# A graph-attention kernel: the attention transposed by VectorE and DMA instead of TensorE, with the maximum and the exponentials moved to the end of the turn

## What is computed

```python
# layer 0: attention, 8 heads of 64 units, per graph
h = max(layernorm(x), 0)
feats = einsum('bnf,hfu->bhnu', h, W)
dense = e_self[..., :, None] + e_neigh[..., None, :]
dense = leaky_relu(dense, 0.2) + NEG_BIG * (1.0 - A[:, None])
att = softmax(dense, axis=-1)
x = x + relu(einsum('bhij,bhju->bhiu', att, feats) + b)
# layer 1: two hypergraph convolutions
h = max(layernorm(x), 0)
r = relu(hypergraph_conv(h, adj, W1, b1)); r = layer_norm(r, gamma, beta)
x = x + (hypergraph_conv(r, adj, W2, b2) + h)
# hypergraph_conv: Dn * H (Be * H^T (x W^T)) + b, H = (adj != 0)
```

## Time and profile before

| | us |
|---|---|
| median of 3 runs (lowest, highest) | 2488.3 (2486.27, 2489.66) |
| profiled execution: time | 2479.36 |
| profiled execution: span, first to last instruction | 2477.6 |
| PE busy | 2419.2 (98%) |
| DVE busy | 1976.4 (80%) |
| ACT busy | 1763.3 (71%) |
| POOL busy | 1368.0 (55%) |

### The profile page before, as it was taken

How to read it: one execution, slowest core, us unless ns; L and a number is a source line. 1 busy time by engine, 2 the same in 40 slices (tenths; PEclk the granted TensorE clock), 3 DMA queues, 4 the chain that set the end, 5 groups by cost and what they waited for, 6 DMA issues and landing times.

```text
span 2477.6 us, 50428 instructions
## 1 busy us (share of the span) xinstructions
PE 2419.2 (98%) x14004; PEld 2101.6 (85%) x14004; DVE 1976.4 (80%) x4373; ACT 1763.3 (71%) x4489; POOL 1368.0 (55%) x1549
## 2 busy tenths in 40 slices
PE   5799999999999999999999999999999999999997
PEld 3688888888888888888888888888888888888886
DVE  3888888888888888888888888888888888888884
ACT  2677777777777777777777777777777777777774
POOL 2465555565565565565555555555555556556543
PEclk8899999999999999999999999999999999999999
DMA  5344454455445445445445445445454444445442
GB/s 206 95 139 138 136 140 137 134 140 140 134 139 141 134 139 141 134 138 142 132 138 143 131 139 143 125 145 139 128 142 137 134 138 138 137 137 138 138 113 72
DMA packets 656793, 336.69 MB, mean 136 GB/s; under 512 B 554752, under 2 KB 571136, under 8 KB 656768
## 3 DMA queue, kind: packets, MB, share of 16 engines
q1 hardware_dynamic: 636256, 298.64, 43.5%
q10 hardware_dynamic: 20512, 37.76, 4.3%
HBM read 235.03 MB, written 101.26 MB: 136 GB/s over the span
## 4 chain that ended last, share of the span: by engine, by line
PE 95%; DMA 2%; DVE 1%; issue 1%; ACT 1%; POOL 0%; SPq 0%; POOLq 0%; DVEq 0%; ACTq 0%
PE p_w1a L853 15%; PE p_w1a L858 14%; PE p_w1a L854 14%; PE p_att L927 9%; PE p_w1b L854 5%; PE p_w1b L858 5%; PE p_w1b L853 5%; PE p_w1b L957 5%; PE p_att L907 4%; PE p_fa L849 3%; PE p_fa L847 3%; PE p_fa L848 3%; PE p_fb L847 2%; PE p_fb L848 2%; PE p_fb L849 2%; PE p_tb L847 1%
## 5 line engine op out<-in xcount | busy, mean ns | idle before, releaser
L338 POOL TENSOR_TENSOR u<-u,mask 128x1024 f32<-128x1024 f32 x128 | 306.6, 2395 | 761.4 <-DMA u<-en_rows 761.4
L438 ACT ACTIVATE att<-u,shifts 128x128 f32<-128x128 f32 x1024 | 402.3, 393 | 133.0 <-DVE shifts L740 131.6
L853 PE MATMUL p_w1a<-W_hi,rT_hi 128*128 128x512 f32 x1024 | 416.8, 407 | 1.5 <-ACT rT_hi L561 1.5
L854 PE MATMUL p_w1a<-W_lo,rT_hi 128*128 128x512 f32 x1024 | 405.9, 396 | 0.0
L439 ACT ACTIVATE att_low<-u,shifts 128x128 f32<-128x128 f32 x1024 | 399.6, 390 | 0.0
L731 DVE TENSOR_REDUCE neg_max<-u 128x8 f32<-128x1024 f32 x128 | 156.1, 1220 | 149.9 <-POOL u L338 149.9
L858 PE MATMUL p_w1a<-W_hi,rT_lo 128*128 128x512 f32 x1024 | 259.5, 395 | 0.0
L392 POOL TENSOR_TENSOR z_lo<-raw,z_hi 128x512 fp32r<-128x512 f32 x128 | 165.7, 1294 | 154.9 <-ACT z_hi L547 154.9
L927 PE MATMUL p_att<-feats,attT 128*128 128x65 f32 x2048 | 243.1, 272 | 3.1 <-ACT attT L483 3.1
L927 PEld LDWEIGHTS p_att<-feats,attT 128*128 128x128 f32 x2048 | 239.5, 192 | 3.9 <-ACT attT L483 3.9
L547 ACT ACTIVATE z_hi<-raw 128x512 fp32r<-128x512 f32 x128 | 81.1, 634 | 221.6 <-DVE raw L797 221.6
(11 more groups left out here) (121 smaller groups left out, 6759.7 us busy)
## 6 DMA issues: line engine op xcount, KB each, us to landing
u<-en_rows SPq DMA_DIRECT2D x130, 576.0 KB, 3.6
r_blocks<-raw SPq DMA_DIRECT2D x128, 512.0 KB, 2.6
raw<-r_blocks SPq DMA_DIRECT2D x512, 128.0 KB, 3.2
xT_in<-in_xT SPq DMA_DIRECT2D x128, 256.0 KB, 3.9
out<-raw SPq DMA_DIRECT2D x128, 256.0 KB, 2.0
x_in<-in_x ACTq DMA_DIRECT2D x124, 256.0 KB, 3.6
adj_in<-in_adj SPq DMA_DIRECT2D x128, 128.0 KB, 2.5
en_rows<-eT SPq DMA_DIRECT2D x520, 1.1 KB
```

Source lines behind the costliest of these rows:

```text
L338: nc.gpsimd.tensor_tensor(u[:, g.slot(2), 0:HEADS, :], u[:, g.slot(2), 0:HEADS, :], mask[:, :].unsqueeze(1).broadcast_to([P, HEADS, N]), A ...
L438: nc.scalar.activation(att[:, i, :], u[:, g.slot(2), i, :], ACT.Exp, bias=shifts[:, 0, i:i + 1])
L853: mm(dst, hi, w_hi, start=first, stop=False)
L854: mm(dst, hi, w_lo, start=False, stop=False)
```

## The change

The attention of a graph is no longer transposed by PE. DVE transposes all of `att` in 32 x 32 blocks into `attB` (a region of `raw` that otherwise takes the unread result of ACT's square), SP writes that to the DRAM scratch `att_blocks` and loads it back by four DMAs into `attT`, in the shape of the round trip that r already makes. The eight PE transposes and ACT's copy out of PSUM are gone. On SP the write stands at the end of a turn, behind the loads of `rT`, and the four loads stand in the next turn behind `adj_in` and in front of `en_rows`.

On DVE the output and norm of t+1 stand directly behind `rB`; behind them come the new transpose and only then the maximum. `larger` is one instruction for all heads, in front of `rB`. `G_rs` moves from DVE to ACT, behind h. On ACT all sixteen exponentials of t+3 stand at the end of the turn, behind `h0`, which moves there too; `hg_hi` goes in front of `z_hi`. On POOL `rs1`, `beT` and `G_lo` go in front of `rest`. The scores, the mask, the maximum and the features run one turn earlier (t+3 and t+5 in place of t+2 and t+4; features t+4), so AHEAD is 6 and `feats` has four slots. The row of `x` is loaded twice, once for the statistics (`x_in`) and once for the residual (`x_res`).

```diff
-AHEAD = 5
+AHEAD = 6
...
-        x_in = sb("x_in", [P, 4, D])
+        x_in = sb("x_in", [P, 2, D])
+        x_res = sb("x_res", [P, 2, D])
...
+        att_blocks = nc.dram_tensor("att_blocks", [P, HEADS * N], F32, kind="Internal").ap()
+
+        def attB(g):
+
+            return raw[:, 1, 0:DH] if g.loop is None and g.base < 2 else dev
...
-                g = t.plus(4)
+                g = t.plus(5)
                 if g.within(NG) and (g.loop is not None or g.base >= 2):
                     load_xT(g)
                 if t.plus(5).within(NG) and (t.loop is not None or t.base >= -1):
                     load_adj(t.plus(5))
+                g = t.plus(1)
+                if g.within(NG):
+
+                    sp.wait_ge(s_attB_out, g.count(per=16))
+                    for c in range(4):
+                        sp.dma_start(attT[32 * c:32 * (c + 1), :, :].rearrange("a k (q b) -> a k q b", b=32),
+                                     att_blocks.rearrange("(q a) (k c b) -> c a k q b", q=4, c=4, b=32)[c]).then_inc(s_attT, 16)
+                g = t.plus(5)
...
+                g = t.plus(2)
+                if g.within(NG):
+
+                    sp.wait_ge(s_attB, g.count())
+                    sp.dma_start(att_blocks[:, :], attB(g)).then_inc(s_attB_out, 16)
...
-                    if g.plus(2).within(NG):
-                        pool.wait_ge(s_shifts, g.plus(2).count())
+                    if g.plus(3).within(NG):
+                        pool.wait_ge(s_shifts, g.plus(3).count())
...
-            def exps(g, half):
+            def exps(g):
 
                 act.wait_ge(s_shifts, g.count())
                 if g.has(1):
-                    act.wait_ge(s_attT, g.count(1))
-                    act.wait_ge(s_att, g.count(1, per=2))
-                for i in range(half * HH, (half + 1) * HH):
+                    act.wait_ge(s_attB, g.count(1))
+                    act.wait_ge(s_att, g.count(1))
...
             def turn(t):
-                if t.plus(1).within(NG):
-
-                    exps(t.plus(1), 1)
...
-                g = t.plus(1)
-                if g.within(NG):
-
-                    act.wait_ge(s_attT, g.count())
-                    if g.has(1):
-                        act.wait_ge(s_o, g.count(1))
-                    nc.scalar.activation(attT[:, :, :].rearrange("p h n -> p (h n)"), p_att[:, :],
...
+                        act.wait_ge(s_attB_out, g.plus(1).count(per=16) if g.plus(1).within(NG) else g.count(per=16))
                     nc.scalar.activation(dev, r, ACT.Square, bias=nm2[:, :], accum_out=sq2[:, :]).then_inc(s_sq2, 1)
...
-                if t.plus(2).within(NG):
-
-                    exps(t.plus(2), 0)
-                g = t.plus(5)
-                if g.within(NG) and (g.loop is not None or g.base >= 4):
-
-                    act.wait_ge(s_x1, g.count(4))
+
+                def row(g):
                     n = g.base if g.loop is None else g.loop * UNROLL + g.base
-                    act.dma_start(x_in[:, g.slot(4), :], x[bass.ds(n, 1), :, :].rearrange("a p d -> p (a d)")).then_inc(s_in[g.slot(4)], 16)
+                    return x[bass.ds(n, 1), :, :].rearrange("a p d -> p (a d)")
+
+                g = t.plus(7)
+                if g.within(NG) and (g.loop is not None or g.base >= 2):
+
+                    act.wait_ge(s_stats0, g.count(2))
+                    act.dma_start(x_in[:, g.slot(2), :], row(g)).then_inc(s_xin[g.slot(2)], 16)
+                g = t.plus(3)
+                if g.within(NG):
+
+                    if g.has(2):
+                        act.wait_ge(s_x1, g.count(2))
+                    act.dma_start(x_res[:, g.slot(2), :], row(g)).then_inc(s_res[g.slot(2)], 16)
...
+                    act.wait_ge(s_G_sb, g.count())
+                    act.wait_ge(s_rs1, g.count())
+                    if g.has(1):
+                        act.wait_ge(s_hg, g.count(1))
+                    nc.scalar.activation(G_rs[:, :], G[:, g.slot(4), 0:N], ACT.Copy, scale=rs1[:, :]).then_inc(s_G_rs, 1)
...
+                g = t.plus(5)
+                if g.within(NG):
+
+                    act.wait_ge(s_xc, g.count())
+                    if g.has(1):
+                        act.wait_ge(s_feats, g.count(1))
+                    nc.scalar.activation(h0[:, :, 0, :], xc[:, :, :], ACT.Relu).then_inc(s_h0_hi, 1)
+                if t.plus(3).within(NG):
+
+                    exps(t.plus(3))
...
-            def larger(g, half):
-
-                dve.wait_ge(s_exp, g.count(per=2) - 1 + half)
-                heads = slice(half * HH, (half + 1) * HH)
-                nc.vector.tensor_tensor(att[:, heads, :], att[:, heads, :], att_low[:, heads, :], ALU.max).then_inc(s_att, 1)
+            def larger(g):
+
+                dve.wait_ge(s_exp, g.count())
+                nc.vector.tensor_tensor(att[:, :, :], att[:, :, :], att_low[:, :, :], ALU.max).then_inc(s_att, 1)
...
-                if t.plus(1).within(NG):
-                    larger(t.plus(1), 1)
-                g = t.plus(3)
+                g = t.plus(4)
...
+                if t.plus(2).within(NG):
+                    larger(t.plus(2))
...
-                g = t.plus(2)
-                if g.within(NG):
-
-                    dve.wait_ge(s_u, g.count())
-                    nc.vector.reduce_max(neg_max[:, :], u[:, g.slot(2), 0:HEADS, :], X, negate=True).then_inc(s_max, 1)
...
-                    nc.vector.scalar_tensor_tensor(x1[:, s, :], o_sc, 0.0, x_in[:, g.slot(4), :],
+                    dve.wait_ge(s_res[s], g.uses(2, 16))
+                    nc.vector.scalar_tensor_tensor(x1[:, s, :], o_sc, 0.0, x_res[:, s, :],
...
-                    dve.wait_ge(s_G_sb, g.count())
-                    if g.has(1):
-                        dve.wait_ge(s_hg, g.count(1))
-                    dve.wait_ge(s_rs1, g.count())
-                    nc.vector.tensor_scalar(G_rs[:, :], G[:, g.slot(4), 0:N], rs1[:, :], None, ALU.mult).then_inc(s_G_rs, 1)
...
-                if t.plus(2).within(NG):
-                    larger(t.plus(2), 0)
+                g = t.plus(2)
+                if g.within(NG):
+
+                    dve.wait_ge(s_att, g.count())
+                    if g.base == 0:
+                        dve.wait_ge(k_lo1, 1)
+                    if g.has(1):
+                        dve.wait_ge(s_attT, g.count(1, per=64))
+                    if t.within(NG):
+                        dve.wait_ge(s_sq2, t.count())
+                    nc.vector.transpose(attB(g), att[:, :, :].rearrange("p h n -> p (h n)")).then_inc(s_attB, 1)
+                g = t.plus(3)
+                if g.within(NG):
+
+                    dve.wait_ge(s_u, g.count())
+                    nc.vector.reduce_max(neg_max[:, :], u[:, g.slot(2), 0:HEADS, :], X, negate=True).then_inc(s_max, 1)
...
-                g = t.plus(1)
-                if g.within(NG):
-
-                    pe.wait_ge(s_att, g.count(per=2))
-                    if g.has(1):
-                        pe.wait_ge(s_osc, g.count(1))
-                    for i in range(HEADS):
-                        last = nc.tensor.transpose(p_att[:, i * N:(i + 1) * N], att[:, i, :], ident[:, :])
-                    last.then_inc(s_attT, 1)
...
-                    pe.wait_ge(s_attT_sb, g.count())
+                    pe.wait_ge(s_attT, g.count(per=64))
+                    if g.has(1):
+                        pe.wait_ge(s_osc, g.count(1))
                     pe.wait_ge(s_feats_sb, g.count(per=2))
                     for i in range(HEADS):
-                        last = mm(p_o[:, i // HH, i % HH, :], attT[:, i, :], feats[:, g.slot(2), i, :], start=True, stop=True)
+                        last = mm(p_o[:, i // HH, i % HH, :], attT[:, i, :], feats[:, g.slot(4), i, :], start=True, stop=True)
```

More of the change, by code:

```diff
@@ L167, in gnn_two_layers @@
         s_in = [sem(f"s_in{i}") for i in range(4)]
+        s_xin = [sem(f"s_xin{i}") for i in range(2)]
+        s_res = [sem(f"s_res{i}") for i in range(2)]
         s_xT = [sem(f"s_xT{i}") for i in range(2)]
@@ L182, in gnn_two_layers @@
         s_mask, s_max, s_neg_s, s_neg_m, s_shifts, s_att = (sem("s_" + n) for n in ("mask", "max", "neg_s", "neg_m", "shifts", "att"))
-        s_exp, s_attT, s_attT_sb, s_o, s_rden, s_osc, s_x1 = (sem("s_" + n) for n in ("exp", "attT", "attT_sb", "o", "rden", "osc", "x1"))
+        s_exp, s_attB, s_attB_out, s_attT, s_o, s_rden, s_osc, s_x1 = (sem("s_" + n) for n in ("exp", "attB", "attB_out", "attT", "o", "rden", "osc", "x1"))
         s_inc, s_sizes, s_row, s_cnt1, s_inv0, s_inv, s_beT, s_G, s_G_sb = (sem("s_" + n) for n in ("inc", "sizes", "row", "cnt1", "inv0", "inv", "beT", "G", "G_sb"))
@@ L304, in setup_rest @@
                 load_last_piece()
-            turns(sp, turn, NG, {-3: setup_rest})
+            turns(sp, turn, NG, {-4: setup_rest})
             for i in range(2):
@@ L538, in turn @@
                     nc.scalar.activation(h[:, g.slot(2), :], x1[:, g.slot(2), :], ACT.Relu, bias=nm1[:, :]).then_inc(s_h, 1)
```

(13 more changed lines are left out.)

90 lines of the change are left out of this document (40 added, 50 removed).

## The result

The changed kernel takes **2648.4 us** (median of 4 runs, 2642.7 to 2658.9), the kernel before 2487.3 us beside it (2485.0 to 2489.7): a ratio of 1.0653, with an interval of 1.0618 to 1.0688. The forecast was 2413, and 2520 the upper end of its range; the time is that of rival (4), 2648.

A forecast was written before the change was run, and what follows sets the result against it. PE was taken as the bound, 18.59 us a turn; without transposes, and with SP's loop, 17.9. 2479.4 - 127 x 0.69 + 13 = 2405, plus 8.9 for the median: 2413 us; own range 2378 to 2451, eight in ten 2378 to 2520.

The forecast's parts named there:

- rival (4): SP's chain: `attB` and `attT` each pay 1.9 us more, a turn is 19.75 us, 2648 us in all; slower, chance 0.20.
- Transposes off PE: PE's chain: the eight transposes go and nothing replaces them, a turn falls from 18.59 to 17.72 us, at most 110 us.
- rival (1): PE stays the sole bound at 17.72 us a turn, with no fill: 2378 us, the forecast's lower end; no separate chance given.
- rival 3: DVE becomes the bound if its idle time stays 2.5 us: 18.6 us a turn, 2501 us; chance 0.08.
- fill: Start of the kernel: one more turn before the first hidden product, charged 13 us, from 0 to 20.
- 19-fold price: `attT`'s load: a DMA copy with transposing strides 19 times slower, 24 us for 5.06, time about 3580; under one in a hundred.
- The new loop: SP's round trips, POOL's u and hg close a loop over two turns: 35.15 to 36.45 us, 17.6 to 18.2 a turn.
- R: The end of `rB` in a turn, when `r_blocks` is issued; the prediction counts SP's and POOL's times from it.
- The first term: On SP, from R to the issue of the loads of `rT`: 2.62 us, as in the earlier trace.
- The third term: On SP, from `attT`'s issue to u's: 5.07 us, made of `en_rows` issues 2.81 + 1.37 and 0.89 to be known.
- The last 12.1 to 12.3 us, hg to R: Last part of the loop, from hg's start to the end of the next `rB`, by PE 12.1 or ACT 12.3 us.
- `attT` covered: The attention product's wait: `attT` lands at R + 14.0 to 14.6, needed near R + 15.9, covered by 1.3 to 1.9 us.

The follow-up runs named there:

- e4: Changed kernel with one of the four loads of `attT`, the rest of the transposed attention left out: 2378.6 us, ratio 0.9576.
- e1: Changed kernel with the eight transposes back on PE and ACT's copy, no round trip of the attention through DRAM: 2486.0 us, ratio 1.0015.
- e5: Changed kernel, same transfers moved: DVE transposes behind `rB`, `att_blocks` written before the wait for `r_blocks`, `attT` loaded right behind `rT`: 2502.8 us, ratio 1.0091.
- e8: Changed kernel with two of the four loads of `attT`, the other half of the transposed attention left out: 2400.5 us, ratio 0.9681.
- e10: Changed kernel with five more matmuls a turn on PE in front of hg, their result overwritten: 2571.8 us, ratio 1.0386.
- e3: Changed kernel with the writes of `en_rows` issued on SP in front of the loads of `attT`: 2600.0 us, ratio 1.0471.
- e11: Changed kernel with the write of `out` moved on SP from in front of `r_blocks` to behind the loads of `rT`: 2661.5 us, ratio 1.0770.
- e12: Changed kernel with ACT's load of `x_in` moved later in the turn, behind h0: 2685.0 us, ratio 1.0811.
- e2: Changed kernel with `rs2`, `rs1`, `beT` and `G_lo` in front of u and xc on POOL: 2616.0 us, ratio 1.0539.
- e6: e5 with `rs2`, `rs1`, `beT` and `G_lo` in front of u and xc on POOL, as in e2: 2854.5 us, ratio 1.1513.
- e9: e5 with three of the eight heads' exponentials moved in front of `rT_hi` on ACT: 2426.6 us, ratio 0.9791.

## Why the prediction was wrong, point by point

- **Transposes off PE, 0.87 us a turn: right.** With PE as the bound (e4) a turn is 17.74 us from the first `r_blocks` to the last, 0.91 less than before. That the time, 2378.6, meets the 2378 of rival (1) is luck: e4 pays 14 us of fill, and rival (1) had none.
- **DVE: right.** `larger` over 1024 columns takes 1.21 us (1.25 predicted), the new transpose 1.25; 16.1 to 16.5 us are busy in a turn, and DVE isn't the bound (rival 3 falls).
- **New order, fill: right.** The order alone is worth 1.0015 (e1); the fill was charged 13 us and measured 13.4. The 19-fold price of such a load, given under one chance in a hundred, did not come: the Trainium skill (VectorE: DVE Perf Modes, The three transpose paths) warns of it, and each of `attT`'s loads of 128 KB landed in a median of 3.6 us, those of `rT` in 3.0.
- **The new loop: its path was right, its size wrong, and here the forecast failed.** The step is the one that brings POOL to u at "R + 17.9 to 19.0". Term by term, in the turn shown and the next: `rT` issued at 4.90 and 4.36 behind R for 2.62; `attT` 7.12 and 6.85 behind `rT` for 6.3 to 6.9; u 6.35 and 6.82 behind `attT` for 5.07; POOL's start 3.87 and 4.71 later for 3.94. The sum is 22.24 and 22.74. Over the 95 turns the medians of the four terms are 4.36, 6.61, 6.60 and 4.45, and of their sum 22.0. The first term gives 1.7 to 2.3 us of the excess. I had taken it over unchanged from the earlier trace rows, because nothing was added between R and `rT`. But what stands *ahead* of R had come nearer: I charged each new transfer for its own wait and not for what it does to the first link of the next turn. e4, e5 and e8 show that term at 2.9 us where u has a lead of about 4 us. The load of `x_in` had come to R as well: 4.7 us behind it before, within 0.8 us of it now; e1, with u 6.1 us ahead, has 3.00. The third term gives another 1.3 to 1.8: SP waits 1.93 us a turn for `en_rows`, whose writes stand behind `attT`, where 0.89 was charged. The four terms add up to R + 17.9 to 18.5; the last half us, up to 19.0, has no working.
- **The last 12.1 to 12.3 us, hg to R, were priced at full clock and without a wait for `rT`.** They took 13.38 and 13.75. In the turn of the 13.38 the mean clock is 0.92. In that of the 13.75 it is 1.00, and ACT waits 1.80 us for `rT` in front of `rT_hi`: the late `r_blocks` acts there through the loop within one turn that e5 shows. Over the 95 turns this stretch is 12.63 on average, 13.47 in the 26 turns with the low clock and 12.32 in the others. A loop in which PE waits can cost more than the wait: e10 gives some 67 us for that part.
- **Rival (4) has the mechanism and the time; its working does not fit in detail.** It put the extra on `attB` and `attT`, 1.9 us each. The runs put most of it on `r_blocks` and `en_rows`, and the part behind hg on top. The 1.9 us itself was not the price of `rT` alone: in e1 `xT_in` stands behind `rT` as before and lands in 3.1 us, not 3.9. That its loop of 39.5 us comes so near the measured mean (2 x 19.87) is partly luck: the two turns shown add up to 41.4, and others are shorter.
- **`attT` covered: nearly right.** 25 waits of the attention product in 127 turns, 24.6 us; it becomes the late one only where `en_rows` is put first (e3).
- **The chance.** The loop came out at 17.6 to 18.2 us a turn by my own sum, around PE's 17.72, with three round trips in it. At 0.20 the slower case was too low: an estimate that lands so close to the bound, with terms that can feed back on each other, is a case near even.

What stays open: how the rest of the loss divides among the links, since `out` and `x_in`, each moved, only changed the link that pays (e11, e12). No run makes `x_in` wait for the issue of `r_blocks`, so what those turns cost isn't measured.

## What to carry to other kernels

When a round trip is added to a queue, write down the queue's whole turn, and ask for each link which transfers now stand close ahead of it, on any queue, the old links too; a chain that comes round to itself grows by more than what was put in. A transfer that nobody needs soon should be issued where the queue waits anyway, not in front of the next link: with the same bytes the change loses 161 us in one place and 23 in the other. And look at what each in-order engine does between the landing and the next issue: the exponentials of three heads, moved in front of a wait, gave 74 us.

## What the runs showed of the hardware

- **A write's landing depends on what was issued just before it, on its own queue and on the other.** From the issue of `r_blocks` (512 KB) to the first load behind its landing it is 2.6 us before, 2.9 where u is 4 us ahead, 4.7 to 4.8 where it is less than 2 ahead (12 turns of e2, 39 of the changed kernel; 4.9 in 60 of e12), and 4.0 where `x_in` (256 KB, ACT's queue) is 0.2 to 0.4 us ahead and u more than 4 (49 turns of e6). `out` (256 KB) lands in 2.0 us before and 4.4 in the changed kernel. The Trainium skill (DMA: Bandwidth & Descriptors, Queues, rings and completion order) says that a queue's descriptors are consumed in ring order on each DMA engine; the medians with u ahead agree with it, and the turns with `x_in` ahead show such a price between two queues too.
- **TensorE's clock after an idle stretch.** Behind 2.24 us without a matmul, hg took 2.05 us where the next one took 1.05, and the features just after it took 0.21 to 0.23 us each for 0.12 to 0.13. The granted clock is 0.50 from 1212.5 to 1215.8, the lower of the two levels, 1.2 GHz; the mean of the turn is 0.92. With five matmuls a turn added in front of hg (e10) the mean from 500 to 1000 us is 1.00.
- **The DMA engines' mean load wasn't the limit.** They were busy for 0.75 of the time in the changed kernel and for 0.86, at 214 GB/s, in e9.
